# Row-sum reciprocals of a background top-k attention two steps later, their spreading three steps later

## The chip, the cores and the metric

The kernel runs on one core of one Trainium2 chip. The metric is the device time of one execution in microseconds. Before the change it was 5967.7 us, the median of three runs (5962.17 to 5971.76). The engines are named as the profile names them: PE multiplies matrices, DVE and POOL work on vectors, ACT applies activation functions and copies, SP issues most transfers.

## The reference

Two transformer layers on four batches of 1024 tokens with 256 features, in float32. Each layer is an attention and a feed-forward part, both modulated by a condition vector. Cut to what matters:

```
x = L0_attn_x                                       # (4, 1024, 256)
h = layernorm(x) * (1 + ca) + sa
x = x + ga * topk_attention(h)                      # layer 0, 16 heads of 16
h = layernorm(x) * (1 + cb) + sb
x = x + gb * top1_experts(h)                        # 8 experts, all computed, one kept
h = layernorm(x) * (1 + ca1) + sa1
x = x + ga1 * wide_attention(h)                     # layer 1, 16 heads of 64
h = layernorm(x) * (1 + cb1) + sb1
x = x + gb1 * block(h)     # causal attention (16 heads of 16), then top-2 of 8 experts, both residual

topk_attention: scores = q @ k.T / 4, causal; the 32 largest of each row are kept;
                softmax over those; out = probs @ v; y = out @ Wo.T + bo
```

The change touches only the last division of `topk_attention`'s softmax: the values are summed with exponentials that are not yet normalised, and the result is divided by the sum of each row afterwards.

## The kernel before

Each engine has a program of its own, written out in order; semaphores tie them together, and no scheduler moves anything. For each batch `b` the order is: projection and expert feed-forward of layer 0, then the wide attention (`wide`), its projection and the preparation of the next attention (`prep`), the causal attention (`flip`), routing (`route`) and 23 tiles of experts (`moe`).

The top-k attention of the **next** batch, `topk(b + 1)`, runs beside the stages of batch `b`, as a background. The top-k attention of batch 0 runs alone at the start, and batch 3 has no background. It has 64 steps. Step `p` treats one head of one pair of row tiles (1152 columns of scores in all): PE makes the scores, ACT copies them (`ssb0`), DVE finds the 32 largest by four rounds of `max` and three of `match_replace`, ACT takes the exponentials, POOL multiplies by the mask of kept entries (`select`), PE transposes, ACT copies (`prT0`), and PE multiplies with the values for two steps at once (`values`), 16 columns and one of ones, which gives the row sums.

Every engine's part is a Python generator that yields once per **tick**. Seven ticks make a step: `p, r = divmod(k, 7)`. At tick `k` DVE works on step `p - 1`, PE transposes step `p - 2` or `p - 3`, and so on. So work for step 63 still runs at ticks with `p` above 64: DVE ends at tick 455, and the product with the values of step 63 is issued at tick 463 (`p = 66, r = 1`).

After every 16 steps (group `g`, four heads) the row sums are turned into factors: ACT sends them by four small DMAs from `oall0` into `rsb0` (`sums_columns`, `p = 18 + 16 g, r = 2`), DVE takes 32 reciprocals per row (L1530, `r = 5` of the same `p`), PE spreads them over the rows in two halves of 32 matmuls (L495, `p = 19 + 16 g, r = 0`), ACT copies each half from PSUM into `rbc0` (L1164), and POOL multiplies `oall0` (L1878). There is one `rbc0`, so ACT's second copy waits until POOL has multiplied the first half, and POOL does that after the `select` that stands ahead of it.

How many ticks run where is set by `Pace`. Each stage has points, at which every engine advances its generator to the same tick:

```
STAGES = (("wide", 8 * 17, 0.51), ("prep", 12, 0.04), ("flip", 8 + 48, 0.22), ("route", 6, 0.04), ("moe", 23, 0.19))
weight = [4 if name == "wide" and i % 17 == 0 else 1 for i in range(points)]
self.at[name, i] = round(TK.TICKS * (done + share * sum(weight[:i + 1]) / sum(weight)))
```

With 472 ticks the stages end at ticks 241, 260, 363, 382 and 472. `TICKS` is therefore both the length of the background and its speed: a tick's place among the points is its number as a share of `TICKS`.

In `moe`, tile `j` is: turn rows, multiply with the first weights (L787), transpose (L795), multiply with the second (L803). After the last tile its result is stored, POOL gathers rows, and DVE normalises the next tokens (L1425), for which SP loads `x` after the last store.

## Time and profile before

| | |
|---|---|
| median of three runs | 5967.7 us |
| the profiled execution, its own time | 5970.14 us |
| its span | 5968.3 us |
| busy share of PE, DVE, ACT, POOL | 76%, 69%, 46%, 32% |
| mean granted clock of PE | 0.862 |

The page's first part gives each engine's busy time over the whole span, an average over stages with different limits. The lines of the program then tell where a stage begins and ends, since each stage has lines of its own, and batch 3, which has no background, shows how long the same stage takes alone. The timeline shows single instructions with the idle time before them and what ended it.

### The profile page before, as it was taken

To read this page: it belongs to the slowest core of one execution; us is meant where nothing else is said; L and a number is where in the kernel's file an instruction comes from. 1 tells how busy PE (TensorE), PEld (TensorE's weight loads), DVE (VectorE), ACT (ScalarE), POOL (GpSimd) and SP (SyncE) were. 2 spreads that over 40 slices of the span, in tenths; PEclk is the share of its full clock that TensorE was granted. 3 is DMA by queue.
4 is the path that set the end of the run, shared out by engine and by line. 5 is a ranking of instruction groups with operands and counts; after the bars stand their busy time and mean duration, and the time that the engine had idled before them with its cause. 6 is when DMAs were issued, how large, how long until landed. Compare 5 with 4: busy or idle time off the path is not lost. (4 is left out here: it accounts for less than half of the span.)

```text
span 5968.3 us, 83328 instructions
## 1 busy us (share of the span) xinstructions
PE 4526.2 (76%) x30341; PEld 2886.9 (48%) x30341; DVE 4103.4 (69%) x8455; ACT 2762.3 (46%) x6047; POOL 1903.4 (32%) x1563
## 2 busy tenths in 40 slices
PE   4444578988677778888777678989777686999776
PEld 2333345656434454666533454656533453666334
DVE  5999957877786757778787656877788555222630
ACT  2334324666253633666345451666445360554333
POOL 2555512444322521443333430434333331000001
PEclk7666689999787889999888788999988798999888
DMA  3000001000201120000221121000031101000312
GB/s 123 11 11 25 1 22 25 18 13 15 52 17 71 45 90 21 14 15 10 48 32 63 42 65 58 13 13 13 15 62 37 62 28 49 17 10 10 63 62 72
DMA packets 113333, 213.59 MB, mean 36 GB/s; under 512 B 25728, under 2 KB 70632, under 8 KB 109552
## 3 DMA queue, kind: packets, MB, share of 16 engines
q1 hardware_dynamic: 104736, 190.94, 11.7%
q0 software_dynamic: 6144, 16.79, 0.9%
q8 instruction: 247, 4.05, 0.3%
q14 instruction: 158, 1.29, 0.1%
q10 hardware_dynamic: 2048, 0.53, 0.0%
HBM read 154.38 MB, written 49.73 MB: 34 GB/s over the span
## 5 line engine op out<-in xcount | busy, mean ns | idle before, releaser
L1492 DVE MAX8 vals<-work 128x8 f32<-128x128 f32 (+7 forms) x1536 | 1080.2, 743 | 0.4
L1866 POOL TENSOR_SCALAR keep<-ssb,vals 128x128 bf16<-128x128 f32 (+7 forms) x512 | 875.3, 1721 | 0.0
L469 PE MATMUL ring<-ident,pr 128*128 128x128 f32 x2304 | 475.9, 325 | 436.8 <-POOL pr L1871 361.4
L1853 POOL TENSOR_TENSOR pool_step<-ones 128x2 f32<-128x2 f32 x256 | 49.6, 194 | 2325.8 <-DVE vals L1492 2317.2
L1506 DVE MATCH_REPLACE8 work<-vals,work 128x128 f32<-128x128 f32 (+7 forms) x1024 | 750.8, 739 | 0.0
L576 PE MATMUL pA<-SC 128*128 128x512 f32 (+3 forms) x1536 | 623.5, 515 | 105.7 <-ACT SC L1204 53.4
L1871 POOL TENSOR_TENSOR pr<-keep,pr 128x128 f32<-128x128 bf16 (+7 forms) x512 | 647.1, 1284 | 1.2 <-ACT pr L1137 1.2
L469 PEld LDWEIGHTS ring<-ident,pr 128*128 128x128 f32 x2304 | 320.3, 165 | 602.4 <-POOL pr L1871 386.5
L1492 DVE MAX8 vals<-ssb 128x8 f32<-128x128 f32 (+7 forms) x512 | 363.0, 750 | 331.2 <-ACT ssb L1131 315.3
L1621 DVE TENSOR_REDUCE nmax<-pA 128x1 f32<-128x1024 f32 (+7 forms) x512 | 384.6, 751 | 297.3 <-PE pA L577 286.3
L1143 ACT ACTIVATE prT<-ring 128x512 f32<-128x512 f32 (+1 forms) x768 | 382.1, 500 | 419.9 <-PE ring L469 418.2
L1204 ACT ACTIVATE SC<-pA,nmax 128x1024 f32<-128x1024 f32 (+7 forms) x512 | 380.6, 743 | 202.9 <-DVE nmax L1621 202.0
L1131 ACT ACTIVATE ssb<-ring 128x512 f32<-128x512 f32 (+3 forms) x768 | 379.6, 496 | 188.3 <-PE ring L461 161.2
L1137 ACT ACTIVATE pr<-ssb,nmx 128x128 f32<-128x128 f32 (+7 forms) x512 | 367.9, 768 | 185.7 <-DVE nmx L1499 148.6
L1653 DVE TENSOR_REDUCE nmx<-pA 128x1 f32<-128x896 f32 (+7 forms) x512 | 359.1, 750 | 80.9 <-PE pA L667 78.7
L1213 ACT ACTIVATE SC<-ring 128x512 f32<-128x512 f32 (+3 forms) x768 | 348.8, 491 | 123.0 <-PE ring L585 117.9
L1280 ACT ACTIVATE SC<-ring 128x512 f32<-128x512 f32 (+3 forms) x768 | 326.6, 497 | 161.0 <-PE ring L699 100.6
L576 PEld LDWEIGHTS pA<-SC 128*128 128x128 f32 x1536 | 260.3, 194 | 289.5 <-issue 143.7
L1506 DVE MATCH_REPLACE8 work<-vals,ssb 128x128 f32<-128x128 f32 (+7 forms) x512 | 380.1, 748 | 0.0
L484 PE MATMUL ring<-prT,vall 128*32 128x128 f32 x4608 | 338.4, 312 | 48.0 <-ACT prT L1143 47.5
L585 PE MATMUL ring<-ident,SC 128*128 128x128 f32 x2304 | 342.5, 276 | 19.6 <-ACT SC L1204 16.8
L1846 POOL TENSOR_TENSOR rstd<-ve,mhalf 128x4 f32<-128x4 f32 x48 | 50.3, 1050 | 946.3 <-DVE ve L1412 946.3
(225 smaller groups left out, 8263.9 us busy)
## 6 DMA issues: line engine op xcount, KB each, us to landing
SC<-in_w SPq DMA_DIRECT2D x64, 512.0 KB, 7.0
stage<-parts SPq DMA_DIRECT2D x384, 64.0 KB, 2.4
parts<-SC SPq DMA_DIRECT2D x72, 256.0 KB, 4.2
SC<-parts SPq DMA_DIRECT2D x144, 128.0 KB, 7.7
SC<-in_wqkv SPq DMA_DIRECT2D x32, 384.0 KB, 3.0
rows_out<-SC SPq DMA_DIRECT2D x92, 128.0 KB, 1.7
SC<-rows_in SPq DMA_DIRECT2D x20, 512.0 KB, 3.9
SC<-in_ffn_we SPq DMA_DIRECT2D x4, 2048.0 KB, 10.1
```

Source lines behind the costliest of these rows:

```text
L469: mm = pe.transpose(r[:, blk % 4 * P:blk % 4 * P + P], pr0[:, p % 2, blk * P:blk * P + P], ident[:, :])
L576: pe.matmul(p[:, lo:hi], qm[:, j, i * P:i * P + P], kT[:, lo:hi], start=True, stop=(hi < w))
L1131: act.activation(ssb0[:, p % 2, col:col + k1 - k0], r[:, 0:k1 - k0], ACT.Copy).then_inc(s_re, 1)
L1137: act.activation(pr0[:, p % 2, lo:hi], ssb0[:, p % 2, lo:hi], ACT.Exp, bias=nmx0[:, p % 2, i:i + 1]).then_inc(s["e"], 1)
L1143: act.activation(prT0[:, p % 2, 4 * c:4 * c + n, :].rearrange("p a n -> p (a n)"), r[:, 0:n * P], ACT.Copy).then_inc(s_re, 1)
L1204: act.activation(pr[:, u % 2, 0:w], pA[(u + 1) % 2][:, 0:w], ACT.Exp, bias=nmax[:, u % 4:u % 4 + 1], accum_out=rsum[:, G % 2, u:u + 1]).th ...
L1492: m = v.max(vals0[:, y, i, 8 * n:8 * n + 8], src[:, lo:hi])
L1506: done[i] = cht.mark(v.match_replace(out=work0[:, lo:hi], in_to_replace=vals0[:, y, i, 8 * n:8 * n + 8], in_values=src[:, lo:hi], imm_valu ...
L1621: v.tensor_reduce(nmax[:, u % 4:u % 4 + 1], pA[(u + 1) % 2][:, 0:w], AX, ALU.max, negate=True).then_inc(s["mx"], 1)
L1653: v.tensor_reduce(nmx[:, j, i:i + 1], pA[c % 2][:, 0:(i + 1) * P], AX, ALU.max, negate=True)\
L1866: pool.tensor_scalar(keep0[:, lo:hi], ssb0[:, p % 2, lo:hi], vals0[:, p % 2, i, TOPK - 1:TOPK], None, ALU.is_ge).then_inc(s["k"], 1)
L1871: pool.tensor_tensor(pr0[:, p % 2, lo:hi], keep0[:, lo:hi], pr0[:, p % 2, lo:hi], ALU.mult).then_inc(s["p"], 1)
```

## The change

The reciprocals move from `p = 18 + 16 g` to `p = 20 + 16 g` (still `r = 5`), the spreading and normalising from `p = 19 + 16 g` to `p = 22 + 16 g` (still `r = 0`), on all four engines that take part. The DMAs of the sums stay at `p = 18 + 16 g, r = 2`. Since the last spreading is now at tick 490, `TICKS` goes from 472 to 493, and the stages end at ticks 251, 271, 380, 399 and 493.

```
--- before.py
+++ after.py
@@ -36,7 +36,7 @@
 
     TILES = ((0, 7), (1, 6), (2, 5), (3, 4))
     STEPS = 64
-    TICKS = 7 * 67 + 3
+    TICKS = 7 * 70 + 3
 
     def __init__(self):
         self.w = 9 * P
@@ -505,8 +505,8 @@
                         turn(p - 2, r - 5)
                     if r == 0 and 0 <= p - 3 < 64:
                         turn(p - 3, 2)
-                    if r == 0 and p >= 19 and (p - 19) % 16 == 0:
-                        spread((p - 19) // 16)
+                    if r == 0 and p >= 22 and (p - 22) % 16 == 0:
+                        spread((p - 22) // 16)
                     if r >= 4 and p < 64:
                         scores(p, r - 4)
                     yield
@@ -1171,8 +1171,8 @@
                         turned(p - 2, r - 5)
                     if r == 0 and 0 <= p - 3 < 64:
                         turned(p - 3, 2)
-                    if r == 0 and p >= 19 and (p - 19) % 16 == 0:
-                        spread((p - 19) // 16)
+                    if r == 0 and p >= 22 and (p - 22) % 16 == 0:
+                        spread((p - 22) // 16)
                     if r == 2 and p >= 18 and (p - 18) % 16 == 0:
                         sums_columns((p - 18) // 16)
                     if r == 2 and 0 <= p - 1 < 64:
@@ -1523,8 +1523,8 @@
                             maxima(p - 1, r // 2)
                         else:
                             replace(p - 1, r // 2)
-                    if r == 5 and p >= 18 and (p - 18) % 16 == 0:
-                        g = (p - 18) // 16
+                    if r == 5 and p >= 20 and (p - 20) % 16 == 0:
+                        g = (p - 20) // 16
                         v.wait_ge(s["sd"], (b * 4 + g + 1) * 64)
                         rows = slice(32 * g, 32 * g + 32)
                         v.reciprocal(rinv0[rows, :], rsb0[rows, :]).then_inc(s["ri"], 1)
@@ -1881,8 +1881,8 @@
 
                 for k in range(TK.TICKS):
                     p, r = divmod(k, 7)
-                    if r == 0 and p >= 19 and (p - 19) % 16 == 0:
-                        normalise((p - 19) // 16)
+                    if r == 0 and p >= 22 and (p - 22) % 16 == 0:
+                        normalise((p - 22) // 16)
                     if r == 6 and 0 <= p - 1 < 64:
                         select(p - 1)
                         chosen[0] = p
```

What this does to the order on an engine shows where stages end. First ACT at the end of the wide attention of batch 0, where L1204 is the last exponential of the wide heads and L1197 copies their factors. Before:

```order
L1190 ACTIVATE Z<-ring 128x128
L1150 ACTIVATE oall<-ring 64x256
L1156 DMA rsb<-oall 8x1x128 x4
L1137 ACTIVATE pr<-ssb,nmx 128x128
L1137 ACTIVATE pr<-ssb,nmx 128x1024
L1190 ACTIVATE Z<-ring 128x128
L1197 ACTIVATE SC<-ring 128x512 x2
```

Now:

```order
L1204 ACTIVATE SC,rsum<-pA,nmax 128x256
L1213 ACTIVATE SC<-ring 128x256
L1131 ACTIVATE ssb<-ring 128x256
L1213 ACTIVATE SC<-ring 128x256
L1190 ACTIVATE Z<-ring 128x128
L1143 ACTIVATE prT<-ring 128x512
L1131 ACTIVATE ssb<-ring 128x512
L1190 ACTIVATE Z<-ring 128x128
L1197 ACTIVATE SC<-ring 128x512 x2
```

The four DMAs of group 1's sums and the exponentials of step 33 have moved ahead, into the last group of the wide attention; copies of scores and transposes of later steps stand in their place.

Second, ACT at the end of the causal attention of batch 0; L1280 is its last exponential, L1256 and L1263 begin its own closing chain. Before:

```order
L1280 ACTIVATE SC<-ring 128x256 x4
L1131 ACTIVATE ssb<-ring 128x256
L1280 ACTIVATE SC<-ring 128x128 x4
L1143 ACTIVATE prT<-ring 128x512
L1131 ACTIVATE ssb<-ring 128x512
L1256 ACTIVATE hT<-pV 128x512
L1263 DMA rsb<-hT 8x1x128 x4
```

Now:

```order
L1280 ACTIVATE SC<-ring 128x128 x4
L1143 ACTIVATE prT<-ring 128x128
L1164 ACTIVATE rbc<-ring 128x512 x2
L1150 ACTIVATE oall<-ring 64x2x128
L1256 ACTIVATE hT<-pV 128x512
L1263 DMA rsb<-hT 8x1x128 x4
```

The two copies of group 2's factors (L1164), which stood three steps of the causal attention earlier, are now the last thing ahead of its closing chain.

Third, ACT at the last expert tiles of batch 0; L1306, L1310 and L1317 belong to the tiles. Before:

```order
L1150 ACTIVATE oall<-ring 64x256
L1306 ACTIVATE hT<-pA 128x512
L1310 ACTIVATE hT<-ring 128x512
L1317 ACTIVATE SC<-pA 128x256
L1156 DMA rsb<-oall 8x1x128 x4
L1310 ACTIVATE hT<-ring 128x512
L1317 ACTIVATE SC<-pA 128x256
L1164 ACTIVATE rbc<-ring 128x512 x2
L1317 ACTIVATE SC<-pA 128x256
```

Now:

```order
L1150 ACTIVATE oall<-ring 64x256
L1300 ACTIVATE SC<-ring,lnw 128x128 x2
L1306 ACTIVATE hT<-pA 128x512
L1310 ACTIVATE hT<-ring 128x512
L1317 ACTIVATE SC<-pA 128x256
L1156 DMA rsb<-oall 8x1x128 x4
...
L1310 ACTIVATE hT<-ring 128x512
L1317 ACTIVATE SC<-pA 128x256
L1164 ACTIVATE rbc<-ring 128x512 x2
L1317 ACTIVATE SC<-pA 128x256
```

The copy of the last values (L1150) and the DMAs of the last sums have moved five tiles ahead, while the copies of the last factors (L1164) still stand right before the last tile's result.

## Rows read from the trace of the kernel before

**Rows 1.** The page's first line: span and instructions.

```profile
span 5968.3 us, 83328 instructions
```

**Rows 2.** Waits, whole span: waiter, releaser, total us, times, longest us.

```profile
DVE rinv L1530 <- DMA rsb<-oall: 92.1, 4, 26.2
ACT rbc L1164 <- POOL oall L1878: 62.7, 16, 6.3
```

**Rows 3.** By line: count, min/median/max ns, first to last start us, forms.

```profile
L576 PE MATMUL pA<-SC x384: 271/590/1222, 943.9 to 1475.5; 128*128 128x512 f32 x96, 128*128 128x128 f32 x32, 128*128 128x384 f32 x32, 128*128 128x256 f32 x32
L576 PE MATMUL pA<-SC x384: 272/591/697, 5097.5 to 5484.2; 128*128 128x512 f32 x96, 128*128 128x128 f32 x32, 128*128 128x384 f32 x32, 128*128 128x256 f32 x32
L1653 DVE TENSOR_REDUCE nmx<-pA x128: 267/806/1224, 1589.4 to 1817.0; 128x1 f32<-128x128 f32 x16, 128x1 f32<-128x256 f32 x16, 128x1 f32<-128x384 f32 x16, 128x1 f32<-128x512 f32 x16
L714 PE MATMUL pV<-SC x384: 272/592/1063, 1644.7 to 1884.4; 128*32 128x512 f32 x96, 128*32 128x384 f32 x32, 128*32 128x256 f32 x32, 128*32 128x128 f32 x32
L1653 DVE TENSOR_REDUCE nmx<-pA x128: 280/752/1225, 5574.2 to 5716.1; 128x1 f32<-128x128 f32 x16, 128x1 f32<-128x256 f32 x16, 128x1 f32<-128x384 f32 x16, 128x1 f32<-128x512 f32 x16
L714 PE MATMUL pV<-SC x384: 272/552/618, 5609.8 to 5757.2; 128*32 128x512 f32 x96, 128*32 128x384 f32 x32, 128*32 128x256 f32 x32, 128*32 128x128 f32 x32
L803 PE MATMUL pA<-SC,hT x184: 379/379/796, 1987.8 to 2152.3; 128*128 x184
L803 PE MATMUL pA<-SC,hT x184: 379/379/382, 5846.2 to 5933.4; 128*128 x184
```

**Rows 4.** Timeline, PE, last expert tiles: start us, us, what, [idle <-releaser].

```profile
2142.64 1.89 PE L803 MATMUL pA<-SC,hT 128*128 x8
2147.18 3.18 PE L495 MATMUL ring<-rinv,ident 128*32 128x128 f32 x64 [2.65 <-DVE rinv L1530]
2150.30 2.39 PE L803 MATMUL pA<-SC,hT 128*128 x8
5930.16 3.62 PE L803 MATMUL pA<-SC,hT 128*128 x16
```

**Rows 5.** Timeline, DVE, across the end of the experts of batch 0.

```profile
2146.18 0.95 DVE L1530 RECIPROCAL rinv<-rsb 32x128 f32<-32x128 f32 x1 [24.49 <-DMA rsb<-oall]
2159.63 1.41 DVE L1425 BATCH_NORM_STATS2 st<-SC 128x6 f32<-128x256 f32 x4 [12.50 <-DMA SC<-in_x]
```

**Rows 6.** Line L1530 in the first 800 us, and its engine's idle time.

```profile
L1530 DVE RECIPROCAL rinv<-rsb x4: 930/943/949, 272.9 to 776.9; 32x128 f32<-32x128 f32 x4
  DMA rsb<-oall: 17.0, 1
```

**Rows 7.** Line L1137 during batch 0's experts, then ACT's timeline there.

```profile
L1137 ACT ACT_TABLE_LOAD  x10: 1283/1283/1283, 1990.1 to 2119.3; - x10
...
2118.90 0.38 ACT L1150 ACTIVATE oall<-ring 64x256 f32<-64x256 f32 x1 [1.72 <-PE ring L484]
2119.29 1.28 ACT L1137 ACT_TABLE_LOAD   x1
2120.59 1.44 ACT L1137 ACTIVATE pr<-ssb,nmx 128x512 f32<-128x512 f32 x2
```

**Rows 8.** Timeline, end of the wide attention of batch 0: ACT, then PE.

```profile
1485.08 2.63 ACTq L1156 DMA_DIRECT2D rsb<-oall  x4
1487.76 1.44 ACT L1137 ACTIVATE pr<-ssb,nmx 128x128 f32<-128x128 f32 x2 [2.71 <-issue]
1489.39 1.08 ACT L1197 ACTIVATE SC<-ring 128x512 f32<-128x512 f32 x2
...
1492.94 4.24 PE L521 MATMUL pA<-SC 128*128 128x256 f32 x12 [5.76 <-POOL Z L1896]
```

**Rows 9.** Timeline, end of the causal attention of batch 0: PE, then DVE.

```profile
1873.64 1.96 PE L495 MATMUL ring<-rinv,ident 128*32 128x128 f32 x64 [0.44 <-ACT prT L1143]
...
1893.49 0.95 DVE L1666 RECIPROCAL rinv<-rsb 32x128 f32<-32x128 f32 x1 [10.97 <-DMA rsb<-hT]
```

**Rows 10.** Line L1492 in the first 800 us, where top-k runs alone.

```profile
L1492 DVE MAX8 vals<-ssb x128: 294/752/1210, 87.8 to 750.6; 128x8 f32<-128x128 f32 x16, 128x8 f32<-128x1024 f32 x16, 128x8 f32<-128x256 f32 x16, 128x8 f32<-128x896 f32 x16
```

More of the change, by code:

```diff
@@ L38 @@
     STEPS = 64
-    TICKS = 7 * 67 + 3
+    TICKS = 7 * 70 + 3
     def __init__(self):
@@ L507, in topk @@
                         turn(p - 3, 2)
-                    if r == 0 and p >= 19 and (p - 19) % 16 == 0:
-                        spread((p - 19) // 16)
+                    if r == 0 and p >= 22 and (p - 22) % 16 == 0:
+                        spread((p - 22) // 16)
                     if r >= 4 and p < 64:
@@ L1173, in topk @@
                         turned(p - 3, 2)
-                    if r == 0 and p >= 19 and (p - 19) % 16 == 0:
-                        spread((p - 19) // 16)
+                    if r == 0 and p >= 22 and (p - 22) % 16 == 0:
+                        spread((p - 22) // 16)
                     if r == 2 and p >= 18 and (p - 18) % 16 == 0:
@@ L1525, in topk @@
                             replace(p - 1, r // 2)
-                    if r == 5 and p >= 18 and (p - 18) % 16 == 0:
-                        g = (p - 18) // 16
+                    if r == 5 and p >= 20 and (p - 20) % 16 == 0:
+                        g = (p - 20) // 16
                         v.wait_ge(s["sd"], (b * 4 + g + 1) * 64)
@@ L1883, in topk @@
                     p, r = divmod(k, 7)
-                    if r == 0 and p >= 19 and (p - 19) % 16 == 0:
-                        normalise((p - 19) // 16)
+                    if r == 0 and p >= 22 and (p - 22) % 16 == 0:
+                        normalise((p - 22) // 16)
                     if r == 6 and 0 <= p - 1 < 64:
```

## The prediction, made before the changed kernel ran

> **What bounds the kernel now.** I read the page's first line [rows 1], then the waits, where the lines of the change stand: DVE idles 92.1 us ahead of four of the sixteen reciprocals, waiting for the DMA of the sums, and ACT idles 62.7 us ahead of its second copy of factors, 3.9 us at each of sixteen places, waiting for POOL [rows 2]. The first looks like the prize. The timeline says otherwise: in batch 0 DVE waits 24.49 us ahead of the reciprocal, and its next work, the normalising of the next tokens, then waits another 12.50 us for the load of `x` [rows 5]. DVE has nothing queued behind that reciprocal but work that comes later anyway, so the wait is no price. In the start-up DVE waits 17.0 us for its fourth reciprocal [rows 6]; there are no ticks with DVE work between step 63 and it, so two empty steps more change nothing, and the start-up keeps its time.
>
> What the change does move is the pace. The background costs each stage time, and by the lines' first and last starts one sees how much, batch 0 against batch 3 [rows 3]: the wide attention takes 1475.5 - 943.9 = 531.6 us against 386.7, so 144.9 more for 241 ticks, 0.60 us a tick. The causal attention, from its first row maximum to its last product with values, takes 295.0 against 183.0, so 112.0 more for 103 ticks, 1.09 us a tick. The expert tiles take 164.5 against 87.2, so 77.3 more. The reader is to see that no engine alone sets these prices: DVE needs (750.6 - 87.8) / 63 first searches = 10.5 us a step when it runs alone, that is 1.50 us a tick [rows 10], and all stages pay less than that, because DVE's work lies partly beside PE's.
>
> **The change part by part.** *Ticks.* With 493 for 472 every stage carries 4.4% more ticks, but only ticks up to 463 hold the steps' work. The wide attention gets 10 ticks more, preparing and the causal attention 7 together, routing none, and the experts 17 fewer that hold work. All of this happens three times, in batches 0 to 2.
>
> *Experts.* Of the 77.3 us the last tile is a part by itself: from the end of the product before it (2142.64 + 1.89 = 2144.53) to its own end (2150.30 + 2.39 = 2152.69) it takes 8.16 us, against 3.62 / 2 = 1.81 in batch 3 [rows 4], so 6.35 more. The other 70.95 us are the steps' work. In these tiles stand, before and now, 10 and 7 sets of scores, 12 and 9 sets of transposes, 10 and 8 pairs of exponentials, 74 and 57 ticks of DVE; about 0.77 of the work is left, and 0.23 x 70.95 = 16.3 us go. Bounds: at the least ACT saves two switches to the exponential's table and two back, of 1.283 us each [rows 7], 5.1 us; at the most 3 of 10 steps go, 21 us.
> The Trainium skill, "ScalarE: Activation LUTs", section "What ACT_TABLE_LOAD costs", gives 2.66 us for a switch, a drain of 1.38 us included. In this trace the load starts 0.01 us after the copy ahead of it ends and the exponential 0.02 us after the load [rows 7], so the trace does not show the drain; by the page the least saving would be 10.6 us in place of 5.1.
>
> *The last tile.* PE waits 2.65 us there for the reciprocal, then spreads for 3.18 us [rows 4]. Now the sums are sent five tiles earlier, so the wait goes, while the spreading stays: -2.65 us. What is late next is ACT's pair of copies with POOL between them, which already ends before the last product, so nothing takes its place.
>
> *Wide attention.* 10 ticks at 0.60 are +6.0 us. That is an average; the next tick may cost more, as DVE is the slower engine where the tiles are narrow. Upper end: DVE's 1.50, +15; lower end: half the average, +3. I take the average, the row nearest to it being this stage's own.
>
> *Preparing and causal attention.* 7 ticks at 1.09 are +7.6 us; ends +4 and, at 1.50, +10.5.
>
> *The end of the wide attention.* The sums of group 1 were sent there: 2.63 us of issuing on ACT, then two exponentials, 1.44 us, and only then the copy of the wide factors; PE sat idle 5.76 us for what follows from it [rows 8]. With a copy of values (0.38, as in [rows 7]) that is 4.45 us, and now three copies of some 0.5 us stand there. So up to 2.9 us go; I take -2.5, since the issuing now stands in the middle of the last group, where it may cost some of it. Lower end 0. The sums of group 0 move from between two heads to the start of a group, where PE is busy with projections: between 0 and -2.63 us, taken as -1.
>
> *Spreading of groups 1 and 2.* It moves past other work. Group 1 was spread while the wide projection waited for DVE; it now stands between the two halves of the causal attention's projection, where PE has 1.96 us of spreading [rows 9] and a product of values to do first. Behind it on PE wait the second half's matmuls, on ACT their copies. Ends 0, since SP is still busy sending the first half, and +3.9, twice the spreading; taken +2. Group 2 was spread three points before the end of the causal attention and now is the last point: ACT's two copies with POOL between them stand ahead of the copy that starts the closing chain, whose DMA DVE awaits for 10.97 us [rows 9]. Ends 0 and +6.3, the longest wait of ACT for POOL [rows 2]; taken +2.5, since PE's 1.96 and one round of POOL are new there and some was paid before.
>
> *The rest.* The reciprocals, 0.94 us each [rows 6], only change place; PE, the one engine that waits for them, has two steps more until it needs them. SP's loads of the next heads' operands move with the ticks, and each still stands a whole head, eight steps, ahead of its use. ACT's wait for POOL stays: POOL's normalising still stands right behind a `select`, one tick after DVE's end of a step, so the 62.7 us are not touched.
>
> Sum for one batch: -16.3 - 2.65 + 6.0 + 7.6 - 2.5 - 1 + 2 + 2.5 = -4.4 us, three times -13 us. The profiled execution took 5970.1 us, 2.4 more than the median, so 5957 by it and 5955 by the median of the runs. All terms are small differences, and a difference of 0.2%, 12 us, is what a measurement of this kernel can tell from none.
>
> **The rivals.** *A balance.* A tick added to a full stage costs more than the average tick does. At 1.0 us for the wide attention's 10 and 1.25 for the causal one's 7 the terms are +10 and +8.8, the sum is +0.9 a batch and the time within 3 us of 5968. For it: the engines' work overlaps, and such costs rise with density. Against: ACT and PE have idle time in every stage, and PE alone loses 2.65 us at the last tile.
>
> *DVE becomes the bound, and the kernel is slower.* Where DVE has no slack left, each added tick costs its own 1.50 us [rows 10]. In the wide attention alone that is +15 in place of +6.0, so the sum is +4.6 a batch and the time 5982; in the causal attention too, +10.5 in place of +7.6, it is +7.5 a batch and 5990. It decides from the point at which DVE no longer idles between the row maxima of the wide heads. For it: DVE's 1.50 us a tick is two and a half times what the stage pays now, so little of it may still be uncovered slack. Against: the price now is 0.60, and 4% more work would have to find all of the cover used up.
>
> *The reciprocal's wait was the price after all.* Then 92.1 - 17.0 = 75.1 us [rows 2, 6] would go, and the time be 5893. Against it stands the second wait of 12.50 us [rows 5]. Or the change does not do what it says: the reciprocal of group 3 still meets sums that are not there, because DVE runs ahead of PE in the experts, and PE's wait at the last tile goes alone: 3 x 2.65, 5960, with the shift of ticks worth nothing.
>
> **How the numbers follow.** The forecast, a net gain from the experts' tiles, has a chance of 0.52; its own range is 5931 to 5962, and 0.44 of it lies below 5955.8, the bound of faster. The balance and the empty change have 0.26, between 5956 and 5980, nearly all of it inside 0.2%. DVE as the bound has 0.21, from 5980 on, and the whole wait regained 0.01. So faster 0.45, within 0.2% 0.33, slower 0.22. For 8 in 10 the range reaches from 5931 (the experts' term at its upper end, 21, and the wide attention's at its lower, a further -7.7 a batch) to 5983, the case in which the wide attention alone is bound by DVE.
>
> **What would show it.** Right: the expert tiles of batch 0 take 145 to 148 us in place of 164.5, the last seven near the 87.2 / 22 = 4.0 us a tile of batch 3; PE's wait for the reciprocal at the last tile is gone; there are 8 loads of the exponential's table for 10; the wide attention takes some 538 us less 2 to 3, the causal one about 302. DVE's wait ahead of the reciprocals stays some 60 to 90 us in all, for no gain. Wrong: if the wide attention takes 545 us or more, or the closing chain of the causal attention starts over 5 us later after its last product; the start-up, the feed-forward part and batch 3 must not move at all.

## The result, and the profile after

The changed kernel takes 5931.94 us (median of four runs, 5928.5 to 5934.72), the kernel before 5965.22 in the same comparison. The ratio is 0.9942 (95% interval 0.9927 to 0.9958): 33 us faster, where 13 were predicted. The direction was right, the size was not. The time lies 1 us above the lower end of the stated range, 5931 to 5983.

This is the page's first line, to be read beside [rows 1]:

```profile
span 5930.3 us, 83316 instructions
```

These are the two waits that the change seems to be about, as in [rows 2]:

```profile
DVE rinv L1530 <- DMA rsb<-oall: 90.3, 4, 26.1
ACT rbc L1164 <- POOL oall L1878: 56.8, 16, 6.1
```

DVE waits for the sums as long as before. ACT's wait for POOL is 5.9 us less in all. Neither shows 33 us by its size. These are the lines of the stages in batch 0, as in [rows 3]:

```profile
L576 PE MATMUL pA<-SC x384: 271/590/1054, 943.7 to 1479.2; 128*128 128x512 f32 x96, 128*128 128x128 f32 x32, 128*128 128x384 f32 x32, 128*128 128x256 f32 x32
L1653 DVE TENSOR_REDUCE nmx<-pA x128: 273/748/1225, 1594.9 to 1828.0; 128x1 f32<-128x128 f32 x16, 128x1 f32<-128x256 f32 x16, 128x1 f32<-128x384 f32 x16, 128x1 f32<-128x512 f32 x16
L714 PE MATMUL pV<-SC x384: 272/592/1063, 1651.8 to 1896.9; 128*32 128x512 f32 x96, 128*32 128x384 f32 x32, 128*32 128x256 f32 x32, 128*32 128x128 f32 x32
L803 PE MATMUL pA<-SC,hT x184: 379/379/483, 1994.0 to 2137.6; 128*128 x184
```

The wide attention took 535.5 us (forecast 538 less 2 to 3), the causal one 1896.9 - 1594.9 = 302.0 (about 302), the expert tiles 2137.6 - 1994.0 = 143.6 (145 to 148). Batch 0 is the kindest of the three. In batches 1 and 2 the causal attention takes 302 us too, but there it had taken 291 before, so it costs 11 us more and not 7; the expert tiles take 149 us there. The loads of the exponential's table in the experts are 8, as forecast, for 10 in [rows 7]; the loads back to the experts' own table (L1306) are 9 for 10, where 8 were counted on.

```profile
L1137 ACT ACT_TABLE_LOAD  x8: 1283/1283/1283, 1992.6 to 2088.3; - x8
```

So inside the stages of batch 0 the forecast nearly held. Next come the last tiles, as in [rows 4], and DVE across the end of the experts, as in [rows 5]:

```profile
2132.27 1.89 PE L803 MATMUL pA<-SC,hT 128*128 x8
2134.10 1.95 PE L495 MATMUL ring<-rinv,ident 128*32 128x128 f32 x64
2135.98 1.99 PE L803 MATMUL pA<-SC,hT 128*128 x8
...
2115.52 0.95 DVE L1530 RECIPROCAL rinv<-rsb 32x128 f32<-32x128 f32 x1 [21.91 <-DMA rsb<-oall]
2144.76 1.41 DVE L1425 BATCH_NORM_STATS2 st<-SC 128x6 f32<-128x256 f32 x4 [28.30 <-DMA SC<-in_x]
```

The last tile has no wait for the reciprocal any more, and takes 3.8 us for 8.2. These are the ends of the two attentions, as in [rows 8] and [rows 9]:

```profile
1495.49 4.54 PE L521 MATMUL pA<-SC 128*128 128x256 f32 x12 [3.12 <-POOL Z L1896]
1907.32 0.95 DVE L1666 RECIPROCAL rinv<-rsb 32x128 f32<-32x128 f32 x1 [12.13 <-DMA rsb<-hT]
```

PE idles 3.12 us for 5.76 at the first (-2.6, forecast -2.5), and DVE 12.13 for 10.97 at the second.

For the sum I divided each batch at four marks and took the mean change of batches 0 to 2 against the kernel before, in us. "Between" runs from the last L803 of the batch before to the first L576, "wide" from there to the last L576, "causal" from there to the last L714, "into the experts" from there to the first L803, "experts" to the last L803. For batch 0 "between" is the start-up, from the start of the span: it is 7 us shorter in e7 and e10 and 3 to 4 in e5, e12, e13 and e15, so that half of their "between" or more lies there; in e8 it is 4 us longer.

One trace stands behind each row, and the difference of two traces parts from that of the medians by up to 8 us (most in e5, e10 and e11), so a sum is good to about 3 us a batch. The medians belong to comparisons of their own, in which the kernel before took 5962.0 to 5968.2 us; the ratio is to before in the same comparison (that of the forecast is 5955 / 5967.7). Where medians and ratios give different gains, the ratio's interval decides.

| kernel | between | wide | causal | into the experts | experts | sum of the five | median | ratio |
|---|---|---|---|---|---|---|---|---|
| forecast | 0 | +5.0 | +7.1 | +2.5 | -19.0 | -4.4 | 5955 | 0.998 |
| changed kernel | -2.1 | +3.9 | +10.3 | -7.2 | -18.1 | -13.3 | 5931.9 | 0.9942 |
| e1_pace_only | -2.3 | +7.6 | +13.4 | -8.3 | -15.6 | -5.1 | 5953.6 | 0.998 |
| e2_moves_only | -0.2 | -5.6 | -3.3 | +2.9 | +0.4 | -5.8 | 5948.8 | 0.9971 |
| e3_even_experts | -2.4 | +16.8 | +15.8 | -7.6 | -19.1 | +3.5 | 5972.8 | 1.0016 |
| e4_no_shift | -2.2 | -6.3 | -6.5 | +3.5 | -6.8 | -18.3 | 5918.1 | 0.9927 |
| e5_spread_p20 | -2.3 | -4.7 | -2.0 | +3.3 | +0.1 | -5.7 | 5961.2 | 0.9992 |
| e6_spread_p23 | -1.4 | +0.4 | -0.3 | +1.4 | -1.4 | -1.3 | 5966.9 | 1.0007 |
| e7_after_select | -2.4 | -4.7 | -1.3 | -0.9 | 0.0 | -9.3 | 5941.7 | 0.9967 |
| e8_more_in_experts | -1.1 | -10.1 | -17.7 | -0.3 | +12.5 | -16.6 | 5913.8 | 0.9917 |
| e9_scatter_first | -0.1 | 0.0 | +0.4 | +4.9 | +1.5 | +6.7 | 5990.0 | 1.0042 |
| e10_combined | -4.7 | -5.8 | -0.9 | -0.1 | -6.5 | -18.0 | 5917.5 | 0.992 |
| e11_idle_ticks | -2.4 | -2.2 | +1.2 | -0.2 | -6.2 | -9.9 | 5942.2 | 0.9962 |
| e12_after_clear | -3.1 | +0.4 | +12.2 | -8.8 | -18.4 | -17.6 | 5916.3 | 0.9921 |
| e13_spread_only | -2.9 | +4.7 | +10.5 | -5.6 | -16.7 | -10.0 | 5935.7 | 0.9944 |
| e14_last_early | -2.3 | +4.1 | +7.8 | -5.7 | -18.2 | -14.3 | 5928.2 | 0.9935 |
| e15_clear_early | -3.3 | -0.7 | +11.3 | -8.1 | -19.2 | -20.1 | 5917.0 | 0.9914 |

Of the stretches, the way into the experts has the largest miss: it is 7.2 us shorter, where 2.5 longer was forecast.

### The profile page after: what moved, and what is told of

It reads as the page before. It is cut to its first block and busy times, and to the rows that moved or that the text cites. A ratio compares the mean times of both kernels' runs of the same rounds, so it can differ in the third digit from the quotient of the medians.

```text
span 5930.3 us, 83316 instructions
## 1 busy us (share of the span) xinstructions
PE 4491.5 (76%) x30341; PEld 2890.1 (49%) x30341; DVE 4104.7 (69%) x8455; ACT 2753.8 (46%) x6035; POOL 1908.1 (32%) x1563
## 5 line engine op out<-in xcount | busy, mean ns | idle before, releaser
L1492 DVE MAX8 vals<-work 128x8 f32<-128x128 f32 (+7 forms) x1536 | 1080.7, 743 | 0.4
L469 PE MATMUL ring<-ident,pr 128*128 128x128 f32 x2304 | 490.9, 334 | 423.8 <-POOL pr L1871 372.2
L576 PE MATMUL pA<-SC 128*128 128x512 f32 (+3 forms) x1536 | 615.6, 510 | 82.8 <-DVE SC L1635 42.3
L469 PEld LDWEIGHTS ring<-ident,pr 128*128 128x128 f32 x2304 | 334.8, 171 | 573.4 <-POOL pr L1871 395.5
L1492 DVE MAX8 vals<-ssb 128x8 f32<-128x128 f32 (+7 forms) x512 | 363.0, 750 | 263.7 <-ACT ssb L1131 246.8
L1204 ACT ACTIVATE SC<-pA,nmax 128x1024 f32<-128x1024 f32 (+7 forms) x512 | 380.6, 743 | 188.1 <-DVE nmax L1621 186.4
L1137 ACT ACTIVATE pr<-ssb,nmx 128x128 f32<-128x128 f32 (+7 forms) x512 | 368.2, 769 | 182.9 <-DVE nmx L1499 151.2
L1280 ACT ACTIVATE SC<-ring 128x512 f32<-128x512 f32 (+3 forms) x768 | 326.9, 496 | 162.2 <-PE ring L699 98.9
L576 PEld LDWEIGHTS pA<-SC 128*128 128x128 f32 x1536 | 259.7, 193 | 259.9 <-issue 141.4
L458 PE MATMUL ring<-stage 96*128 96x512 bf16 (+3 forms) x768 | 302.4, 395 | 81.0 <-ACT SC L1213 28.3
## 6 DMA issues: line engine op xcount, KB each, us to landing
SC<-in_ffn_we SPq DMA_DIRECT2D x4, 2048.0 KB, 10.3
```

Source lines behind the costliest of these rows:

```text
L469: mm = pe.transpose(r[:, blk % 4 * P:blk % 4 * P + P], pr0[:, p % 2, blk * P:blk * P + P], ident[:, :])
L576: pe.matmul(p[:, lo:hi], qm[:, j, i * P:i * P + P], kT[:, lo:hi], start=True, stop=(hi < w))
L1204: act.activation(pr[:, u % 2, 0:w], pA[(u + 1) % 2][:, 0:w], ACT.Exp, bias=nmax[:, u % 4:u % 4 + 1], accum_out=rsum[:, G % 2, u:u + 1]).th ...
L1492: m = v.max(vals0[:, y, i, 8 * n:8 * n + 8], src[:, lo:hi])
```

## The experiments

My theory after the result was that the pace alone made the gain. Its rival was that the places of the reciprocals and the spreadings did.

**e1_pace_only.** The kernel before, with one line changed.

```diff
-    TICKS = 7 * 67 + 3
+    TICKS = 7 * 70 + 3
```

> 493 ticks in place of 472, but the reciprocals, the spreading and the normalising stay at their old steps (p = 18 and 19 + 16 g). Theory A (the gain comes from the pace: 17 ticks of background work leave the route and the experts, POOL's scatter meets one select fewer, and the last sums are sent early enough): about the whole gain of the change, -27 to -40 us against before. Rival B (the gain comes from the later reciprocals and spreading, which no longer wait): within 8 us of before.

The ratio is 0.998 (0.9971 to 0.9989). The pace is about a third of the gain, so neither theory holds alone. In this kernel DVE runs into the sums at group 0 too, 5.85 us in each of three batches (here batch 0):

```profile
1215.19 0.94 DVE L1530 RECIPROCAL rinv<-rsb 32x128 f32<-32x128 f32 x1 [5.85 <-DMA rsb<-oall]
```

At group 2, inside the causal attention, ACT's second copy waits for POOL and PE stands idle behind it:

```profile
1859.65 0.60 ACT L1164 ACTIVATE rbc<-ring 128x512 f32<-128x512 f32 x1 [4.64 <-POOL oall L1878]
1860.31 0.34 PE L699 MATMUL ring<-SC 98*128 98x384 bf16 x1 [4.53 <-ACT rbc L1164]
```

**e2_moves_only.** It has 472 ticks, and only the places are changed: these are values of `p`, with `r` as in the changed kernel, and group 3 stays where it was.

```diff
+    INVERT = (20, 36, 52, 66)
+    SPREAD = (22, 38, 54, 67)
```

> 472 ticks as before; the reciprocals and the spreading of groups 0 to 2 are moved as in the change, group 3 stays in its old place. Theory A: within 8 us of before, since no engine on the path waited for these twelve reciprocals. Rival B: -20 to -33 us.

The ratio is 0.9971 (0.996 to 0.9982). The moves, which were priced at about nothing, bring 17 us by themselves. Of the 5.8 us a batch 5.6 stand in the wide attention; what the causal one gains (3.3) is lost again on the way into the experts (2.9).

**e3_even_experts** and **e4_no_shift.** The shares of the stages set by hand: e3 gives the kernel before, at 472 ticks, the changed kernel's ends (251, 271, 380, 399); e4 gives the changed kernel the ends of before (241, 260, 363, 382).

```diff
-    ("wide", 8 * 17, 0.51), ("prep", 12, 0.04), ("flip", 8 + 48, 0.22), ("route", 6, 0.04), ("moe", 23, 0.19)
+    ("wide", 8 * 17, 251 / 472), ("prep", 12, 20 / 472), ("flip", 8 + 48, 109 / 472), ("route", 6, 19 / 472), ("moe", 23, 73 / 472)
...
+    ("wide", 8 * 17, 241 / 493), ("prep", 12, 19 / 493), ("flip", 8 + 48, 103 / 493), ("route", 6, 19 / 493), ("moe", 23, 111 / 493)
```

> 472 ticks and the old steps, but the stages' shares are set so that the wide attention, the preparation, the causal attention and the route get the ticks that the change gives them (251, 20, 109, 19) and the experts the remaining 73, spread over all 23 tiles. Theory A1 (a tick of background costs the experts much the same wherever it stands): the change's gain without the last tile's part, -33 + 3 x 4 = about -20 us. Rival A2 (what pays is that the last seven tiles are empty of background): between 0 and -10 us.

> The changed kernel with 493 ticks and its later steps, but shares that leave the wide attention, the preparation, the causal attention and the route the ticks they had before (241, 19, 103, 19); the experts get 111, so their background work is denser and done by tile 16. Theory A1: only the last tile's wait and DMA issue go, -5 to -13 us. Rival A2: most of the change's gain, -25 us or more.

e3 has a ratio of 1.0016 (1.0007 to 1.0025), e4 one of 0.9927 (0.9913 to 0.994). e4 is 9 us below the changed kernel by the ratios; their intervals overlap a little, but each of its five runs lies under each of the changed kernel's four. The shift of work out of the experts, my main term, is thus no gain in either. What e4 keeps are the 21 further ticks, all in the experts, and the moves. e3 alone does not show what the shift costs: in the traces its wide attention takes 9 us a batch more than that of e1, though both run the same 251 ticks in it. By the formula of `Pace` they differ at 29 of its 136 points, by one tick each, from rounding alone. Which of these points makes the difference stays open; the sums of e3 and e1 must be read with that in mind.

**e5_spread_p20, e6_spread_p23, e7_after_select.** Each is the kernel before at 472 ticks with other ticks for groups 0 to 2, to see what about the place counts. The first lines stand for the same replacement on all four engines.

```diff
-                    if r == 0 and p >= 19 and (p - 19) % 16 == 0:
-                        spread((p - 19) // 16)
+                    if k in TK.SPREAD:
+                        spread(TK.SPREAD.index(k))
...
+    INVERT, SPREAD = (131, 243, 355, 467), (140, 252, 364, 469)     # e5
+    INVERT, SPREAD = (145, 257, 369, 467), (161, 273, 385, 469)     # e6
+    INVERT, SPREAD = (131, 243, 355, 467), (137, 249, 361, 469)     # e7
```

> The kernel before at its own 472 ticks; only the spreading and the normalising of groups 0 to 2 stand one step later (at p = 20, 36, 52, r = 0), the reciprocals where they were. In wide this spread goes from tick 133 to tick 140, point 78: still inside head group 4 (u = 9), but with the reciprocal a step and a half behind it. With all moves alone the stretch from the first L576 to wide's first L521 came down by 5.4, 7.3 and 4.2 us. Theory 'place' (what was won there was that the spread left the middle of a head group): this one still stands in the middle, so wide changes by less than 2 us a batch, and the time stays within 5 us of before. Theory 'wait' (what was won is that nothing waits for the reciprocal or for the sums any more): wide falls by 4 to 7 us a batch, and the time is 10 to 17 us lower.

> As before with 472 ticks; the reciprocals of groups 0 to 2 two steps later, the spreading and the normalising four steps later (p = 23, 39, 55, r = 0). In wide the spread then stands at tick 161, point 89: past the boundary, in the middle of head group 5 (u = 3). The other two go to the causal stage (tick 273) and to the experts (tick 385). Theory 'place' (the spread is cheap only at the boundary of two head groups): wide is no better than before by more than 2 us a batch, the time within 5 us of before or a little higher. Theory 'wait' (any place is good once nothing waits for it): wide falls by 4 to 7 us a batch as with the moves alone, the time is 10 to 20 us lower.

> As before with 472 ticks; reciprocals where they were, the spreading and the normalising of groups 0 to 2 four ticks later, in the same step (p = 19, 35, 51, r = 4): tick 137 in wide, point 76, still in the middle of head group 4 and a whole step away from the boundary, but POOL's select that stood ahead of its normalising at r = 6 of the step before is then some 20 us behind. Theory 'queue' (ACT stalls at the spread because of what POOL and DVE still have to do, and four ticks are enough to be rid of it): wide falls by 4 to 7 us a batch and the time by 10 to 17 us. Theory 'place' (the middle of a head group is what costs): wide within 2 us a batch of before, the time within 5 us.

e5 has a ratio of 0.9992 (0.9983 to 1.0001), e6 of 1.0007 (0.9997 to 1.0016), e7 of 0.9967 (0.9957 to 0.9978). First, this is group 0 in batch 0 of the kernel before: POOL, then ACT, then PE.

```profile
1234.34 3.42 POOL L1866 TENSOR_SCALAR keep<-ssb,vals 128x128 bf16<-128x128 f32 x2
1237.72 2.53 POOL L1871 TENSOR_TENSOR pr<-keep,pr 128x128 f32<-128x128 bf16 x2
1240.20 1.27 POOL L1878 TENSOR_TENSOR oall<-oall,rbc 128x512 f32<-128x512 f32 x1
...
1234.65 0.60 ACT L1164 ACTIVATE rbc<-ring 128x512 f32<-128x512 f32 x1 [0.73 <-PE ring L495]
1241.57 0.60 ACT L1164 ACTIVATE rbc<-ring 128x512 f32<-128x512 f32 x1 [6.32 <-POOL oall L1878]
...
1242.31 0.88 PE L596 MATMUL ring<-SC 128*64 128x128 f32 x12 [4.53 <-ACT rbc L1164]
```

ACT's first copy is done at 1235.25. The second may overwrite `rbc0` only when POOL has multiplied with it, and POOL is at work on the `select` of the tick before (1234.17 to 1240.25). ACT stands still, and PE behind it. This is the same place in e7, where the spreading comes four ticks later:

```profile
1236.55 0.60 ACT L1164 ACTIVATE rbc<-ring 128x512 f32<-128x512 f32 x1 [0.73 <-PE ring L495]
1238.59 0.60 ACT L1164 ACTIVATE rbc<-ring 128x512 f32<-128x512 f32 x1 [1.44 <-POOL oall L1878]
...
1241.10 0.39 PE L458 MATMUL ring<-stage 96*128 96x512 bf16 x1 [0.74 <-ACT SC L1213]
...
ACT rbc L1164 <- POOL oall L1878: 29.8, 16, 3.6
```

POOL's `select` is over, ACT waits 1.44 us, the whole wait falls from 62.7 to 29.8 us, and the time by 25 us by the medians, 20 by the ratio (interval 13 to 26), more than either theory had. In the trace 7 us of it stand in the start-up, where the same spreadings run: ACT waits 3.56 us there for 5.4 to 6.1. In e6 the spreading of group 0 stands as badly as before, in another head group:

```profile
1303.47 0.60 ACT L1164 ACTIVATE rbc<-ring 128x512 f32<-128x512 f32 x1 [6.45 <-POOL oall L1878]
1304.89 2.08 PE L576 MATMUL pA<-SC 128*128 128x512 f32 x2 [5.34 <-ACT SC L1204]
```

e5 also stands in the middle of a head group and right behind a `select`, but ACT comes when that is half done; it waits 3.2 us, PE idles 1.9, and the wide attention gains 4.7. A part is lost again: POOL's multiplications of group 2 fall among its 16 scatter DMAs (L1930: 35.6 us for 32.3), and the way into the experts takes 3.3 us more. The medians show only 5.5 us of gain where the trace shows 14, so how much e5 brings stays unclear.

So "place", in the sense of a head group's boundary, falls with e7, and with the wide attention of e5. The boundary helped e2, where ACT waits 2.6 us and PE not at all, because ACT comes late to it: its first copy ends at 1279.80, and the `select` that began at 1275.01 ends at 1281.10. "Queue" stands.

**e9_scatter_first.** This one is about the way into the experts. POOL's points of the routing stage move behind the scatter.

```diff
                 for i in range(2 * NT):
                     pool.indirect_dma_start(...)
-                    if i % 4 == 3:
-                        at("route", i // 4)
-                for i in range(4, 6):
+                for i in range(6):
                     at("route", i)
```

> The kernel before with one change: POOL issues its 16 scatter DMAs (L1930) in one go and meets the routing stage's first four points after them, not one point after every fourth DMA. In the profile of before the 16 took 32.3 us with two selects of some 6 us between them, in that of after 26.3 us with one. Theory 'scatter' (the shorter routing of after, 2.3 to 4.8 us a batch, and a part of its shorter first tile, are the select that left the scatter): 16 DMAs take 20 to 22 us, the routing and the first tile together are 3 to 8 us shorter a batch, and the time is 9 to 24 us lower. Theory 'ticks' (they are shorter because fewer steps stand there on TensorE; the rows are waited for no less, or PE's own steps wait for POOL's late selects instead): routing and first tile change by less than 2 us a batch, the time by less than 6 us either way.

The ratio is 1.0042 (1.0029 to 1.0056), so it is slower. It went the way of the second theory, far beyond the 6 us that this had allowed. The 16 DMAs took 20.2 us, as expected, but PE waits longer for the `select` that now stands behind them (first the kernel before, then e9):

```profile
1963.80 1.12 PE L469 MATMUL ring<-ident,pr 128*128 128x128 f32 x4 [12.49 <-POOL pr L1871]
1974.18 1.12 PE L778 MATMUL ring<-ident,SC 128*128 128x128 f32 x4 [3.30 <-DMA SC<-rows_in]
1975.78 3.78 PE L787 MATMUL pA<-SC 128*128 x4 [0.49 <-ACT SC L1300]
```

```profile
1963.47 1.12 PE L469 MATMUL ring<-ident,pr 128*128 128x128 f32 x4 [17.30 <-POOL pr L1871]
1982.61 3.78 PE L787 MATMUL pA<-SC 128*128 x4 [4.67 <-ACT SC L1300]
```

From the scatter's first DMA to the first L803 the trace of before counts 51.4 us with four `select`s and 32 transposes of the background, that of after 43.5 us with three and 27; the other two batches are alike within 0.2 us. All kernels with the changed kernel's stage ends have its counts and 43 to 46 us: e1, e3 and e12 to e15. Those with the old ends, e2, e4 to e7, e10 and e11, have the old counts and 51 to 55 us; e8, with four `select`s and 35 transposes, has 51 to 53. This is the changed kernel there:

```profile
1983.01 1.12 PE L469 MATMUL ring<-ident,pr 128*128 128x128 f32 x4 [8.83 <-POOL pr L1871]
1985.73 1.06 PE L778 MATMUL ring<-ident,SC 128*128 128x128 f32 x4
1987.34 1.98 PE L787 MATMUL pA<-SC 128*128 x4 [0.55 <-ACT SC L1300]
```

One step less stands in this stretch, though both have 19 ticks of routing. A `select` stands at one tick of seven: before, the ticks 363 to 385 up to the experts' first point hold four of these, and the ticks 380 to 402 hold three. The first L787 takes 1.98 us for 3.78. The windows show the clock (the stretch, its us, PE's busy time, and, third from the end, the granted clock): before, from the scatter to the first transposes and over the first L787; then after, the same two.

```profile
1936.40:1974.20 37.80, 16.39 (x108) 12.05 (x108) 29.40 (x59) 11.12 (x23) 33.42 (x31) 0.55 0.22 78
1975.80:1979.30 3.50, 3.50 (x4) 1.38 (x5) 1.44 (x3) 1.53 (x2) 1.99 (x3) 0.50 0.00 0
```

```profile
1950.50:1985.70 35.20, 13.30 (x77) 9.96 (x78) 26.68 (x56) 10.01 (x21) 30.57 (x29) 0.60 0.26 90
1987.34:1989.20 1.86, 1.86 (x5) 0.86 (x6) 1.83 (x4) 1.55 (x3) 1.83 (x2) 1.00 0.00 0
```

Before, the products ran at a granted clock of 0.50, that is 1.2 GHz, behind a wait for the rows of 3.30 us; after, transposes of a step and of the rows stood directly ahead, and they ran at 1.00, 2.4 GHz. That is 1.8 of the 8 us, but the order ahead does not decide it alone. In 6 of the 21 batches that have it, over seven kernels, the first L787 takes 3.7 to 3.8 us all the same, and the whole stretch 45 to 46 us for 43.3 to 43.5, as in batch 2 of e13:

```profile
4738.33 1.06 PE L778 MATMUL ring<-ident,SC 128*128 128x128 f32 x4
4739.94 3.78 PE L787 MATMUL pA<-SC 128*128 x4 [0.55 <-ACT SC L1300]
```

Its granted clock is 0.50 there. In all three batches of the changed kernel's trace it was 1.00.

**e8_more_in_experts, e10_combined, e11_idle_ticks, e12_after_clear.** e8 is e4 with stage ends 231, 249, 346 and 365. e10 and e11 have e4's ends; e11 has the steps of before, e10 the spreading of e7. e12 is the changed kernel with a clear spreading, that is one that meets no `select` on POOL. The edits are shortened here.

```diff
+    STAGES: 231 / 493, 18 / 493, 97 / 493, 19 / 493, 128 / 493                     # e8
+    INVERT, SPREAD = (131, 243, 355, 481), (137, 249, 361, 490)   # e10
+    TICKS = 7 * 70 + 3, steps of before                            # e11
+    SPREAD = (151, 263, 375, 490)                                  # e12, was (154, 266, 378, 490)
```

> The changed kernel with its steps and its 493 ticks, but with the stages' ends put by hand at ticks 231, 249, 346, 365 and 493: 17 ticks fewer stand ahead of the experts than in the kernel before (248 to 399 there becomes 346 to 365 here), so the experts hold 128 ticks, 98 of them with work. The same with the ends where the kernel before had them took 5918.1 us. Theory 'a tick costs less in the experts': wide falls by some 6 us a batch against that run (10 ticks at 0.6), preparing and the causal stage by 5 to 9 (7 ticks at 1.09), the experts rise by 5 to 9, and the time is near 5908. Theory 'flat' (a tick costs the same everywhere, what was lost by the shift lay in where the spreading fell): the stages trade one for one, the time within 6 us of 5918. Theory 'the experts are full': they rise by more than 15 us a batch, the time is 5930 or more.

> 493 ticks with the stages' ends where the kernel before had them, and the spreading and normalising of groups 0 to 2 four ticks after their old places (ticks 137, 249 and 361, as in the run at 472 ticks that took 5941.7 us), group 3 at ticks 481 and 490 as in the changed kernel. Theory 'queue' (what a spread costs is ACT's wait for POOL's select, wherever it stands, and this is independent of the idle ticks at the end): ACT's second copy waits 1.4 to 1.6 us everywhere, and both gains add up, 25 us of the one and some 30 of the other, so the time is 5908 to 5915. Theory 'place' (the later spreading at the boundary of two head groups was worth as much): 5916 to 5922, as the run with these stage ends and the later spreading, 5918.1.

> All steps and reciprocals where the kernel before has them; only the count of ticks is 493 with the stages' ends kept at 241, 260, 363 and 382, so that the 21 further ticks all stand in the experts and the last 24 hold no work. Every stage ahead of the experts must be as before within 1 us a batch. Theory 'idle end' (the experts like their steps early, the last tile and what follows it then have none): the experts with their last tile are 6 to 12 us shorter a batch, the time 5930 to 5947. Theory 'moves' (the gain of the later steps is the whole of it): the experts only trade earlier tiles for later ones, the time is within 8 us of before.

> The changed kernel, its pace and its reciprocals kept; only the spreading and the normalising of groups 0 to 2 stand three ticks earlier, in the middle of step 21, 37 and 53 (ticks 151, 263, 375), where POOL's select of the step before is over. In the changed kernel ACT's second copy waits 5.1, 1.8 and 4.0 us there for POOL. Theory 'queue': these waits become 1.4 to 1.6 us, wide falls by 2 to 4 us a batch and the causal stage by 1 to 3, the time is 5911 to 5922. Theory 'place': wide rises, since the spread then stands in the middle of head group 4, and the time is 5932 or more.

e8 has a ratio of 0.9917 (0.9904 to 0.9929), which is "flat": 17 more ticks cost the experts 19 us a batch against e4, and the stages ahead give that back.

e11 has 0.9962 (0.9951 to 0.9974), which is "idle end": with the old steps and the old stage ends, 23 ticks without work at the end (470 to 492) bring 20 us. The last tile takes 1.7 us for 6.5 to 8.2, and what follows up to the wide attentions of batches 1 and 2 is 3.7 and 3.0 us shorter. The last two tiles' products now stand together:

```profile
2140.72 3.62 PE L803 MATMUL pA<-SC,hT 128*128 x16
```

Its wide attention, which was to stay as before within 1 us, is 2.2 us a batch shorter. By another rounding 13 of its 136 points stand one tick further on, and ACT's wait at group 0 is 3.9 to 5.0 us for 6.3. So a part of the 20 us may belong to that wait.

e10 has 0.992 (0.9908 to 0.9932) and is 44 us below before in the same comparison. By the medians e7's 25 and e11's 20 add up; I had put the second at 30 and so expected a lower time. ACT's waits are 1.4 us at every group of batches 0 to 2, as "queue" had them, but the time, 5917.5, lies in the range of "place" and beside the 5918.1 of e4, whose spreading came later. With these stage ends the two kinds of place are worth the same; e7 and e12 are what tells them apart.

e12 has 0.9921 (0.9909 to 0.9934), 12 us better than the changed kernel by the ratios, and all its runs lie under all of the changed kernel's. In group 0 ACT waits 1.44 us for 5.11, and PE 1.14 for 3.31:

```profile
1271.13 0.60 ACT L1164 ACTIVATE rbc<-ring 128x512 f32<-128x512 f32 x1 [5.11 <-POOL oall L1878]
1271.87 1.09 PE L596 MATMUL ring<-SC 128*64 128x128 f32 x16 [3.31 <-ACT rbc L1164]
```

```profile
1257.28 0.60 ACT L1164 ACTIVATE rbc<-ring 128x512 f32<-128x512 f32 x1 [1.44 <-POOL oall L1878]
1258.02 1.53 PE L596 MATMUL ring<-SC 128*64 128x128 f32 x24 [1.14 <-ACT rbc L1164]
```

The first two lines are the changed kernel, the others e12. In its trace the gain stands in the wide attention (-3.5 us a batch against the changed kernel) and in the start-up (-4 us once). The causal attention, which was to fall by 1 to 3 us, takes 1.9 more: at groups 1 and 2 ACT waits less, but PE idles 1.1 and 1.4 us for it, where in the changed kernel it does not idle for it at all. e10 and e12, both with clear spreading, have the old and the new stage ends, and differ by 1 us.

**e13_spread_only, e14_last_early, e15_clear_early.** These ask which of the two moves counts, and of which groups.

```diff
+    if r == 5 and p >= 18 and (p - 18) % 16 == 0:                    # e13: reciprocals back, rest as changed
+    INVERT, SPREAD = (145, 257, 369, 467), (154, 266, 378, 469)      # e14: group 3 back
+    INVERT, SPREAD = (145, 257, 369, 467), (151, 263, 375, 469)      # e15: e14 with clear spreading
```

> The changed kernel with its 493 ticks and its later spreading and normalising, but with all reciprocals at their old ticks (p = 18, 34, 50, 66, r = 5). With the pace alone DVE waited 5.85 us for the sums at the reciprocal of group 0 in the wide attention, three times, and the time was 5953.6; with both moves there is no such wait and it is 5931.9. Theory 'reciprocal' (DVE's wait is what the two later steps save): DVE waits 5 to 6 us again ahead of the reciprocal of group 0, wide is 3 to 5 us a batch longer than in the changed kernel, the time 5941 to 5950. Theory 'spread' (the place of the spreading is the whole of it): DVE's wait comes back but wide stays within 1.5 us a batch of the changed kernel, the time within 5 us of 5932.

> The changed kernel with its 493 ticks and with groups 0 to 2 as it has them, only group 3's reciprocal and spreading stand where the kernel before had them (ticks 467 and 469 of 493), so some four tiles ahead of the last one. Theory 'last tile' (the last spreading costs the last tile 1.95 us on PE and nothing else): the last tile takes 1.7 us in place of 3.8, the time is 4 to 8 us lower, 5924 to 5928. Theory 'wait' (so early, the sums are not there, and PE waits for the reciprocal inside the tiles): PE waits up to 5 us at the spreading, the time is 5930 to 5940.

> The run before this one with the spreading of groups 0 to 2 three ticks earlier, clear of POOL's select (ticks 151, 263, 375). If the three gains are independent (idle ticks at the end, clear spreading, group 3 out of the last tile), this has all of them and is 12 to 16 us below the run before it: 5908 to 5916, about 4 to 6 below the run with the clear spreading alone (5916.3). If group 3's place is worth nothing, it stays within 3 us of that run.

e13 has a ratio of 0.9944 (0.993 to 0.9957), and the changed kernel 0.9942. DVE's wait is back:

```profile
DVE rinv L1530 <- DMA rsb<-oall: 107.1, 7, 24.4
```

The 17 us more of it cost nothing that can be told from none. Beside the pace, the spreading's place is all; the later reciprocals are worth nothing that shows.

e14 has 0.9935 (0.9921 to 0.9949), some 4 us below the changed kernel, which is within the intervals: the last tile takes 1.7 us, an earlier one 7.0 for 4.1, and moving group 3 into the last tile was no gain. e15 has 0.9914 (0.9901 to 0.9928), the lowest ratio of all. Its time, 5917.0, is within 1 us of e12's and not the 4 to 6 below it that three independent gains would have given, so group 3's place is worth nothing that shows here either.

## Why the prediction was right in direction and wrong in size

*The reciprocal's wait is no price*: this was right, and it is shown from both sides. The total stayed at 90.3 us while the time fell by 33, and e13 brings 17 us of the wait back without losing that time.

*Pace and last tile*: the forecast was -16.3 - 2.65 + 6.0 + 7.6 = -5.35 us a batch, and e1 measured -12 us in all, -4 a batch. That the sum held is luck, because two wrong terms offset each other. Preparing and the causal attention cost more (+13.4 in e1 for +7.6). "Routing none" failed: the count of ticks is the same, but a `select` and five transposes fewer stand between the scatter and the first L803, -8 us a batch. My window for the experts began at the first L803, and the experts' first point lies ahead of it, so no term held that stretch. The wide attention (+7.6 for +6.0) and the experts (-15.6 for -19.0) were nearer. As a whole the shift is what the first rival said, a balance, and no net gain: e10 against e12, and e8 against e4, are 1 and 4 us apart. (e3 against before and the changed kernel against e4 lose 7 and 14 us by the medians, but there the spreadings' waits differ too.) What the pace gains is the idle end (e11, 20 us at the most), of which I had priced only the wait at the last tile, 3 x 2.65 = 8 us.

*Spreading and the rest*: this is the step that failed, and it makes the difference to 33 us. I had spreading +2 and +2.5, with the end of wide -2.5 and the sums -1, in sum +1.0 a batch, and wrote that ACT's wait for POOL stays, "so the 62.7 us are not touched". Moving the spreading is worth -22 us from e1 to the changed kernel, -7 a batch, and -17 from before to e2. The total of the wait hardly moved (56.8 us), so the sentence reads true; but I had taken from it that nothing changes.

What the wait costs is set by what ACT has to do for PE when it comes there: 6.32 us of it idled PE for 4.53 in the middle of a wide head group, 2.6 us (e2) did not idle PE at all. The mean of 3.9 us at sixteen places hid this: before, the second copy waits 6.3 us at group 0, 5.6 at group 1 and 1.4 at groups 2 and 3, and 18 of the 62.7 us stand in the start-up. e7, whose only edit is four ticks, shows that this wait was worth 20 to 25 us, a price that my list of rivals did not have.

The term for group 2 at the end of the causal attention was well sized, +2.0 for +2.5. The copy that starts the closing chain now begins 2.43 us after the last product with values ends (1897.17), for 0.43 before (1884.72); first before, then after:

```profile
1885.15 0.61 ACT L1256 ACTIVATE hT<-pV 128x512 f32<-128x512 f32 x1
```

```profile
1899.60 0.58 ACT L1256 ACTIVATE hT<-pV 128x512 f32<-128x512 f32 x1
```

Group 1's +2 does not show: neither before nor after has PE an idle time there that ends with ACT's copy. The -1 for the sums of group 0 was not measured apart.

*The last tile*: the wait went as forecast; the term was -2.65 and measured -4.3, -2.7 and -4.3 in batches 0 to 2. The 1.6 us more in batches 0 and 2 are the clock: the spreading takes 1.95 us for the 3.18 of [rows 4], and the products behind it are shorter too. By the windows, before and after:

```profile
2147.20:2150.30 3.10, 3.10 (x65) 2.71 (x65) 0.00 (x0) 0.60 (x1) 0.92 (x1) 0.58 0.03 8
```

```profile
2134.10:2136.00 1.90, 1.90 (x66) 1.70 (x65) 0.00 (x0) 0.98 (x2) 0.08 (x1) 1.00 0.19 65
```

A granted clock of 0.58 is mostly the lower level, 1.00 the upper. Before, PE idled 2.65 us ahead of the spreading, now it does not. The idle time alone does not decide, though: in batch 1 of the kernel before PE idled just as long, and the spreading took 1.95 us at a granted clock of 1.00:

```profile
3534.70 1.95 PE L495 MATMUL ring<-rinv,ident 128*32 128x128 f32 x64 [2.66 <-DVE rinv L1530]
```

*The end of the wide attention*: PE's idle time went as forecast, -2.6 for -2.5, but the stretch from the last L576 to the first L521 is only 1.1 to 1.5 us shorter. *DVE as the bound* did not come: the wide attention took 3.9 us more, not 15. Batch 3 and the start-up kept their times within 3 us.

*The range* held by luck as well. Its lower end stood for an experts' term of -21 and a wide attention of +3; the time came down to it by the spreading and the way into the experts, which had no such term.

What stays open is how the 7 us a batch between e1 and the changed kernel divide. 3.7 of them stand in the wide attention, where PE's idle time at group 0 went from 5.11 to 3.31, and 3.1 from there to the causal attention's end. In that stretch PE idles 4.53 us at group 2 and 1.46 at group 1 in e1, and not at all for ACT's copies in the changed kernel. But groups 1 and 2 were not moved apart, so the share of each is not shown.

## What to carry to other kernels

Price a wait by what is queued behind the waiter, and look for waits on a buffer that a third engine must first finish with: the costly one here was not the 92 us on DVE but ACT's 62.7 us for POOL, and four ticks of distance from POOL's other work took half of it away (e7). When a schedule is stretched, ask first what stands in its last slots, and which items fall into the short stretches that nothing covers; the average price of a slot says little about either.

## What the runs showed that I had not expected

POOL's scatter DMAs and its `select`s come one behind the other, and each adds its whole time: 20.2 us for 16 DMAs without interruption (1.26 us each) and 6.1 us for a `select`. Putting the DMAs first only moved the wait to PE's transposes (12.49 to 17.30 us) and made the kernel 23 us slower. And a wait on DVE of 5.85 us inside the wide attention, three times a run, cost nothing measurable, on an engine that is busy 69% of the time.
